# A Flamingo block in fp32: the resident operand's transfers issued from ScalarE's queue instead of SyncE's

## The chip, the core and the metric

The kernel runs on one core of one Trainium2 chip. The metric is the device time of one execution in microseconds (us); for each kernel the median of several executions is taken. A core has TensorE (matrix products, weights loaded by PEld), VectorE (DVE), ScalarE (ACT), GpSimd (POOL) and SyncE (SP). Each takes its own instructions strictly in order, and they wait for each other by semaphores. SP computes nothing: before the change every DMA of this kernel is issued from it. An engine that issues a DMA goes on to its next instruction once the transfer is handed over; the data land later and raise a semaphore.

## The reference

One gated cross-attention layer and one gated mixture of rank-16 experts, 16 batches of 128 rows, hidden size 1024, all fp32:

```python
x = x + tanh(g_xattn) * xattn(layernorm(x), ctx)
x = x + tanh(g_ffn) * ffn(layernorm(x))

# xattn: 32 query heads, 8 key/value heads, head size 128
q, k, v = hs @ q_w.T, ctx @ k_w.T, ctx @ v_w.T
q, k = rmsnorm(q, q_norm_w), rmsnorm(k, k_norm_w)
out = softmax(q @ k.T / sqrt(128) + mask) @ v     # per head
return out @ o_w.T

# ffn: top 16 of 64 experts
scores = xf @ Wr.T
gates = softmax of the 16 largest scores, 0 elsewhere
h = einsum('nd,krd->nkr', xf, A)
return einsum('nkr,kdr->nd', h * gates, B) * 2
```

## The kernel before

**Products.** Every large product is a Strassen-Winograd step: seven products of half-size blocks in place of eight. The work is a list of 100 entries, each with seven products, k = 0 to 6 (router entries have four). A product is four steps `at`, and each step three matmuls, since fp32 is split into a high part and a low rest: high by high, high by low, low by high (lines 719 to 721). One operand of an entry is **resident**: seven tiles `t_hi[k]`, `t_lo[k]` of 128 x 2048 numbers, which stay for a whole set of entries. The other is **staged**: `staged` (128 x 7 x 512) is loaded anew for every entry, four of its seven blocks are formed by POOL (`sums`, lines 1662 to 1668), and ACT or POOL (`s_hi`) and DVE (`s_lo`) split it.

**Sets.** There are eleven sets `tau` of resident tiles, so the resident operand is exchanged ten times. The set of an entry: 0 and 1 for entries 0 to 15 (keys and values), 2 and 3 for 16 to 47 (queries, with attention interleaved), 4 to 7 for 50 to 81 (output projection), 8 and 9 for 82 to 91 (router and expert inputs), 10 for 92 to 99 (expert outputs). The exchange happens while entries flow on. In the last entry of a set, `refill(e, k)` (line 384) waits until product k of that entry is done, since this was the last reader of tile k, and issues a 1 MB transfer of the next set's tile into `t_raw[k]`, which lies over `t_lo[k]`. `fill_t` then makes `t_hi[k]` on ACT (line 945, a cast) and `t_lo[k]` on DVE (line 1229, a subtraction). They stand at beats 4, 5, 6, 7, 9, 10 and 11 counted from the start of the last entry, a beat being one product: k = 0 is split while product 4 of the last entry runs. The first entry of the new set waits for `t_lo[k]` before its product k (line 713). There are 10 x 7 = 70 such refills.

**What else SP does.** `stage(e + 1, e)` (line 408) loads the staged operand of the next entry once `s_lo` of this entry is finished; it stands behind beat 1, so behind two refills, and in the query entries in round 1, behind three. Around it SP stores keys, values, combinations (`combos`), transposed rows (`xt`, `x2t`), attention heads and partial sums (`sums_out`), and loads them again. `sums_in` (line 509) waits until the store before has landed. SP's order is written out by hand in the loops from line 602: per beat `refill`, then `stage`, then the rest. In the query entries (line 624) a round is a quarter of an entry; rounds 0 to 3 hold refills 0; 1 and 2; 3 and 4; 5 and 6, each time ahead of `heads_out` and `stage`.

**What ACT does around it.** Keys and values (line 1138), output projection (line 1187) and the later loops: per beat the copies out of PSUM, `fill_s` (line 947, `s_hi` of the next entry at beats 5 and 6), then `fill_t`. In the query entries (line 1159), per round: `heads_copy`, the sums of squares of the queries, `exps`, `probs_high`, then `fill_t`. There `s_hi` is made by POOL.

Of the kernel before, what the change touches and what calls it, by code (L numbers as in the profile page):

```python
# [57 lines left out]
TAUS = 11  # L58
# [175 lines left out]
def program(nc, d, plan, bank, sem, ctx):  # L234

    m = Sbuf(nc)
    t_hi, t_lo, t_raw, s_hi, s_lo = [], [], [], [], []
# [145 lines left out]
    def _(sp):  # L383
        def refill(e, k):
            tau = entries[e].tau
            if plan.last_of_set[tau] != e or tau + 1 == TAUS:
                return
            tau += 1
            sp.wait_ge(prod, plan.prod[e, k])
            if tau in (2, 3):  # L390
                if k == 0:
                    sp.wait_ge(xt_out, 448 * (tau - 1))
                src = d.xt[tau - 2, k].rearrange("p k a c -> p k (a c)")
            elif tau in (8, 9):
                if k == 0:
                    sp.wait_ge(ft_out, 448 * (tau - 7))
                src = d.x2t[tau - 8, k].rearrange("p k a c -> p k (a c)")
            else:
                which = {1: 1, 4: 2, 5: 3, 6: 4, 7: 5, 10: 6}[tau]
                if k == 0:  # L400
                    sp.wait_ge(pc_out, 64 * which)
                if k in (0, 4, 5):
                    src = d.sets[which, {0: 0, 4: 1, 5: 3}[k]].rearrange("p (k c) -> p k c", k=4)
                else:
                    src = d.combos[which, {1: 0, 6: 1, 2: 2, 3: 3}[k]].rearrange("p (k c) -> p k c", k=4)
            sp.dma_start(t_raw[k][:, :, :], src).then_inc(t_in[k], 16)

# [194 lines left out]
        for e in range(KV0, QA0):  # L602
            for j in SEVEN:
                refill(e, entries[e].ks[j])
# [19 lines left out]
        for n in range(34):  # L624
            e = QA0 + n
            for r in range(4):
                if n < 32:
                    for k in ((0,), (1, 2), (3, 4), (5, 6))[r]:
                        refill(e, k)
# [18 lines left out]
        for q in range(32):  # L648
            e = O0 + q
            for j in SEVEN:  # L650
                refill(e, j)
# [17 lines left out]
        for e in range(A0, B0):  # L669
            s, idx = (e - A0) // 5, (e - A0) % 5  # L670
            for j, k in enumerate(entries[e].ks):
                beat = plan.beat0[e] + j
                refill(e, k)
# [267 lines left out]
    def _(act):  # L941
# [4 lines left out]

        def fill_s(e, ks):
# [190 lines left out]
        for e in range(KV0, QA0):  # L1138
            for j in SEVEN:
# [14 lines left out]
                if j == 5:  # L1154
                    key_squares(e, 0)
                    x_seeds(e)
                fill_t(plan.beat0[e] + j)

        for n in range(34):
            e = QA0 + n  # L1160
            for r in range(4):
# [19 lines left out]
                if 0 <= i - 2 < 128:  # L1181
                    probs_high(i - 2)
                for j in SLOT_BEATS[r]:
                    fill_t(plan.beat0[e] + j)
        heads_copy(127)

        for q in range(32):
            e = O0 + q
            for j in SEVEN:
# [7 lines left out]
                fill_s(e + 1, before_next(e, j))  # L1197
                fill_t(plan.beat0[e] + j)
# [620 lines left out]
```

## Time and profile before

| | |
|---|---|
| time, median of 3 executions | 2584.53 us (2575.5 to 2589.01) |
| the profiled execution's own time | 2579.23 us |
| its span in the trace | 2577.4 us |
| PE, DVE, POOL, ACT busy | 90%, 65%, 52%, 45% of the span |
| moved by DMA | 452.81 MB, mean 176 GB/s |
| granted TensorE clock, mean | 0.956 |

The trace is of one execution. Its times are counted from the start of the span. A row of a timeline that stands for several instructions ("x2") gives the first start and the time from there to the last end, waits between them included. The words in brackets are the idle time of the engine before the row and what ended it.

### The profile page before, as it was taken

Reading aid. Unit: us, or ns where it says so; the run is one execution under the profiler, and the core shown is the slowest. Engines: PE = TensorE matmul, PEld = TensorE weight load, DVE = VectorE, ACT = ScalarE, POOL = GpSimd, SP = SyncE. Lnnn points to the kernel's source line nnn. Section 1 sums busy time; section 2 is a strip of 40 time slices with the busy share of each in tenths; the row PEclk is TensorE's granted clock in tenths of the full one; section 3 lists DMA queues with packets and bytes.
Section 4 is the critical chain, followed back from the end, with each engine's and each line's share of the span. In section 5 each row is a group of like instructions: output and inputs, shape, how many; then the busy total and the mean of one; then the engine's idle time right before and its main releaser. Section 6 shows DMA issues by size and latency. Waiting matters only on the chain.

```text
span 2577.4 us, 35293 instructions
## 1 busy us (share of the span) xinstructions
PE 2328.8 (90%) x11384; PEld 1937.0 (75%) x11384; DVE 1664.1 (65%) x2655; ACT 1167.8 (45%) x3739; POOL 1343.0 (52%) x1822
## 2 busy tenths in 40 slices
PE   6997998999999999999996998999997576978899
PEld 4775786888888788888885886877875455756687
DVE  6557557777777787777776336556476555655755
ACT  4445445666666766666666333223231113332321
POOL 6888788555555555655554554322234443344431
PEclk8999999999999999999997999999998787989999
DMA  4788777322233522232334578576575548474754
GB/s 173 249 257 307 239 248 255 106 84 86 91 94 97 191 83 91 87 91 87 99 119 140 205 252 305 197 260 217 201 280 168 180 158 283 129 231 134 241 172 142
DMA packets 265541, 452.81 MB, mean 176 GB/s; under 512 B 14224, under 2 KB 154768, under 8 KB 249488
## 3 DMA queue, kind: packets, MB, share of 16 engines
q1 hardware_dynamic: 265360, 450.55, 52.7%
q8 instruction: 94, 1.54, 0.2%
q14 instruction: 87, 0.71, 0.1%
HBM read 288.49 MB, written 162.00 MB: 175 GB/s over the span
## 4 chain that ended last, share of the span: by engine, by line
PE 61%; DMA 13%; POOL 9%; DVE 9%; issue 4%; SPq 3%; ACT 1%; ACTq 0%; DVEq 0%; POOLq 0%
PE bank L719 16%; PE bank L721 16%; PE bank L720 16%; PE bank L777 4%; DVE s_lo L1229 2%; PE bank L785 2%; PE bank L765 2%; DVE t_lo L1229 2%; DMA gates_of_ranks<-gates_t 2%; SPq L537 2%; DMA x<-x_rows 1%; DVE x_rows L1377 1%; POOL staged L1664 1%; POOL staged L1662 1%; PE bank L800 1%
## 5 line engine op out<-in xcount | busy, mean ns | idle before, releaser
L719 PE MATMUL bank<-t_hi,s_hi 128*128 128x512 f32 x2720 | 1125.9, 414 | 160.2 <-DVE s_lo L1229 91.1
L721 PE MATMUL bank<-t_hi,s_lo 128*128 128x512 f32 x2720 | 1086.3, 399 | 0.0
L720 PE MATMUL bank<-t_lo,s_hi 128*128 128x512 f32 x2720 | 1085.4, 399 | 0.0
L719 PEld LDWEIGHTS bank<-t_hi,s_hi 128*128 128x128 f32 x2720 | 527.4, 194 | 278.8 <-DVE s_lo L1229 100.2
L1229 DVE TENSOR_TENSOR s_lo<-staged,s_hi 128x512 fp32r<-128x512 f32 x676 | 536.6, 838 | 212.8 <-ACT s_hi L954 203.5
L721 PEld LDWEIGHTS bank<-t_hi,s_lo 128*128 128x128 f32 x2720 | 525.8, 193 | 119.3
L720 PEld LDWEIGHTS bank<-t_lo,s_hi 128*128 128x128 f32 x2720 | 528.2, 194 | 94.5
L954 ACT CAST s_hi<-staged 128x512 fp32r<-128x512 f32 x452 | 258.6, 621 | 355.8 <-DMA staged<-heads 156.0
L1662 POOL TENSOR_TENSOR staged<-staged 128x512 f32<-128x512 f32 x96 | 135.3, 1410 | 441.8 <-DMA staged<-heads 249.4
L1243 DVE TENSOR_TENSOR sums<-sums,bank 128x512 f32<-128x512 f32 x184 | 125.1, 682 | 184.4 <-PE bank L721 165.0
L1647 POOL TENSOR_SCALAR q_v<-q_ss 128x4 f32<-128x4 f32 x128 | 44.2, 345 | 368.9 <-ACT q_seed L1038 365.8
L1229 DVE TENSOR_TENSOR t_lo<-t_raw,t_hi 128x2048 fp32r<-128x2048 f32 x77 | 190.5, 2482 | 50.7 <-ACT t_hi L945 41.4
L1339 DVE SCALAR_TENSOR_TENSOR probs<-bank,q_rstd,mask 128x128 f32<-128x128 f32 x512 | 144.1, 344 | 99.8 <-POOL q_rstd L1654 55.5
L1044 ACT ACTIVATE probs<-probs,neg_max 128x128 f32<-128x128 f32 x512 | 197.5, 387 | 15.3 <-DVE neg_max L1343 15.3
L1032 ACT ACTIVATE bank<-bank 128x128 f32<-128x128 f32 x512 | 136.4, 266 | 120.1 <-PE bank L765 120.0
L777 PEld LDWEIGHTS bank<-keys,queries 128*128 128x128 f32 x1024 | 136.9, 196 | 30.7 <-issue 20.4
L1026 ACT COPY heads<-bank 128x512 f32<-128x512 f32 x128 | 75.2, 587 | 178.4 <-PE bank L802 176.9
L777 PE MATMUL bank<-keys,queries 128*128 128x128 f32 x1024 | 139.3, 280 | 18.1 <-DVE probs L1339 18.1
L945 ACT CAST t_hi<-t_raw 128x2048 fp32r<-128x2048 f32 x70 | 132.8, 1907 | 32.4 <-DMA t_raw<-in_sets 22.1
L1664 POOL TENSOR_TENSOR staged<-staged 128x512 f32<-128x512 f32 x96 | 141.8, 1477 | 7.5
L1665 POOL TENSOR_TENSOR staged<-staged 128x512 f32<-128x512 f32 x96 | 144.0, 1500 | 0.0
L1668 POOL TENSOR_TENSOR staged<-staged 128x512 f32<-128x512 f32 x96 | 142.4, 1483 | 0.0
(137 smaller groups left out, 2865.2 us busy)
## 6 DMA issues: line engine op xcount, KB each, us to landing
sums<-sums SPq DMA_DIRECT2D x48, 1280.0 KB, 7.9
heads<-heads SPq DMA_DIRECT2D x128, 256.0 KB, 2.9
t_raw<-combos SPq DMA_DIRECT2D x24, 1024.0 KB, 12.0
staged<-in_w_q SPq DMA_DIRECT2D x32, 768.0 KB, 5.2
staged<-heads SPq DMA_DIRECT2D x32, 768.0 KB, 5.8
t_raw<-in_sets SPq DMA_DIRECT2D x22, 1024.0 KB, 10.1
x_rows<-in_x SPq DMA_DIRECT2D x32, 512.0 KB, 6.6
combo<-in_sets SPq DMA_DIRECT2D x15, 1024.0 KB, 6.4
```

The costliest lines, as they stand in the source:

```text
L719: nc.tensor.matmul(out[:, :], s_hi[w][:, cols], t_hi[k][:, at, :], start=start, stop=False, skip_group_check=True)
L720: nc.tensor.matmul(out[:, :], s_hi[w][:, cols], t_lo[k][:, at, :], start=False, stop=False, skip_group_check=True)
L721: done = nc.tensor.matmul(out[:, :], s_lo[w][:, cols], t_hi[k][:, at, :], start=False, stop=at == 3, skip_group_check=True)
L777: done = nc.tensor.matmul(bank[6][:, b * S:b * S + S], qt[j][:, b, :], kg[blk][:, b, :], start=True, stop=True)
L954: nc.scalar.copy(s_hi[k][:, :], staged[:, k, :]).then_inc(s_hi_done, 1)
L1044: done = nc.scalar.activation(pr[i % 3][:, b, :], pr[i % 3][:, b, :], ACT.Exp, bias=nmax[w][:, b:b + 1], accum_out=rsum[w][:, b:b + 1])
L1229: return nc.vector.tensor_tensor(out, whole, hi.bitcast(FP32), ALU.subtract)
L1339: done = nc.vector.scalar_tensor_tensor(pr[i % 3][:, b, :], bank[6][:, b * S:b * S + S], q_rstd[w][:, b:b + 1], mask[:, :], ALU.mult, ALU.add)
L1662: nc.gpsimd.tensor_tensor(staged[:, 2, :], staged[:, 3, :], staged[:, 6, :], ALU.add).then_inc(s_sum, 1)
L1664: nc.gpsimd.tensor_tensor(staged[:, 1, :], staged[:, 2, :], staged[:, 0, :], ALU.subtract).then_inc(s_sum, 1)
L1665: nc.gpsimd.tensor_tensor(staged[:, 3, :], staged[:, 0, :], staged[:, 3, :], ALU.subtract).then_inc(s_sum, 1)
L1668: nc.gpsimd.tensor_tensor(staged[:, 5, :], staged[:, 4, :], staged[:, 1, :], ALU.subtract).then_inc(s_sum, 1)
```

## The change

`refill` moves from SP's program to ACT's. The same 70 transfers with the same semaphores are issued by `nc.scalar.dma_start`, and the waits ahead of them (for the product, and for k = 0 also for the data's own store) are now ACT's. The place of each call: in the key/value, output and expert loops behind this beat's `fill_s` and right ahead of `fill_t`; in the query loop at the end of each round, behind `probs_high` and ahead of `fill_t`. The four loads of set 0 stay with SP. No computation changes.

```diff
     @block.sync
     def _(sp):
-        def refill(e, k):
-            ...
-            sp.wait_ge(prod, plan.prod[e, k])
-            ...
-            sp.dma_start(t_raw[k][:, :, :], src).then_inc(t_in[k], 16)
...
             for j in SEVEN:
-                refill(e, entries[e].ks[j])
                 if j == 1:
                     stage(e + 1, e)
...
             for r in range(4):
-                if n < 32:
-                    for k in ((0,), (1, 2), (3, 4), (5, 6))[r]:
-                        refill(e, k)
                 heads_out(4 * (n - 2) + r - 1)
...
     @block.scalar
     def _(act):
...
+        def refill(e, k):
+            tau = entries[e].tau
+            if plan.last_of_set[tau] != e or tau + 1 == TAUS:
+                return
+            tau += 1
+            act.wait_ge(prod, plan.prod[e, k])
+            if tau in (2, 3):
+                if k == 0:
+                    act.wait_ge(xt_out, 448 * (tau - 1))
+                src = d.xt[tau - 2, k].rearrange("p k a c -> p k (a c)")
+            ...
+            nc.scalar.dma_start(t_raw[k][:, :, :], src).then_inc(t_in[k], 16)
...
                     x_seeds(e)
+                refill(e, entries[e].ks[j])
                 fill_t(plan.beat0[e] + j)
...
                     probs_high(i - 2)
+                if n < 32:
+                    for k in ((0,), (1, 2), (3, 4), (5, 6))[r]:
+                        refill(e, k)
                 for j in SLOT_BEATS[r]:
                     fill_t(plan.beat0[e] + j)
...
                 fill_s(e + 1, before_next(e, j))
+                refill(e, j)
                 fill_t(plan.beat0[e] + j)
```

The SP queue in entry 31, the last query entry of set 2, before: `staged` is the next entry's operand, `xt` the source of the refills, `product` the semaphore of finished products.

```order
L406 DMA t_raw<-xt 128x2048 [waits product] x2
L485 DMA heads<-heads_172 128x2x256 [waits ot_copied]
L433 DMA staged<-in_w_q 128x3x512 [waits s_lo_done]
L434 DMA staged<-in_w_q 128x512
L406 DMA t_raw<-xt 128x2048 [waits product] x2
L485 DMA heads<-heads_173 128x2x256 [waits ot_copied]
L501 DMA values_raw<-values 128x512 [waits pv_done]
L406 DMA t_raw<-xt 128x2048 [waits product] x2
```

The same stretch of SP in the changed kernel (its line 409 is the old line 433):

```order
L461 DMA heads<-heads_172 128x2x256 [waits ot_copied]
L409 DMA staged<-in_w_q 128x3x512 [waits s_lo_done]
L410 DMA staged<-in_w_q 128x512
L461 DMA heads<-heads_173 128x2x256 [waits ot_copied]
L477 DMA values_raw<-values 128x512 [waits pv_done]
```

Three pairs of refills, each with waits for products, are gone from ahead of the staged load, the head stores and the value load.

ACT in rounds 2 and 3 of the same entry in the changed kernel (`q_ss`, `q_ln`, `q_seed` are the queries' norm, `probs` the softmax):

```order
L939 DMA t_raw<-xt 128x2048 [waits product] x2
L915 CAST t_hi<-t_raw 128x2048 [waits t_in0]
L915 CAST t_hi<-t_raw 128x2048 [waits t_in1]
L1020 COPY heads_172<-bank 128x512 [waits heads_out0,pv_done]
L1009 COPY queries_161<-bank 128x512 [waits s_done,product]
L1026 ACTIVATE bank,q_ss_109<-bank 128x128 [waits qt_done]
L1026 ACTIVATE bank,q_ss_109<-bank 128x128 x3
L1030 ACTIVATE q_ln_111<-q_ss_109,eps 128x4 [waits q_squared]
L1032 ACTIVATE q_seed_113<-q_ln_111 128x4 [waits q_logged]
L1038 ACTIVATE probs_170,row_sum_122<-probs_170,neg_max_120 128x128 [waits s_max]
L1038 ACTIVATE probs_170,row_sum_122<-probs_170,neg_max_120 128x128 x3
L1052 CAST probs_t_hi<-bank 128x512 [waits pv_done,pt_done]
```

The first row is new: refills 3 and 4 with their waits for products 3 and 4 now stand ahead of the casts of tiles 0 and 1 and of the whole of round 3. Another pair, 5 and 6, follows the last row, ahead of the cast of tile 2.

ACT in entry 65, the last one of set 5 (output projection), in the changed kernel:

```order
L939 DMA t_raw<-combos 128x2048 [waits product] x3
L939 DMA t_raw<-in_sets 128x2048 [waits product]
L915 CAST t_hi<-t_raw 128x2048 [waits t_in0]
L948 CAST s_hi<-staged 128x512 [waits staged_in,product]
L948 CAST s_hi<-staged 128x512 [waits s_sum,product]
L939 DMA t_raw<-in_sets 128x2048 [waits product]
L915 CAST t_hi<-t_raw 128x2048 [waits t_in1]
L948 CAST s_hi<-staged 128x512 [waits s_sum,product] x2
L939 DMA t_raw<-combos 128x2048 [waits product]
L915 CAST t_hi<-t_raw 128x2048 [waits t_in2]
```

Before, the casts stood in the same order without the DMA rows. Refill 4 now stands ahead of the cast of tile 0, refill 5 behind two `s_hi` that wait for the staged load and POOL's sum of it, refill 6 behind two more.

## Rows read from the trace of the kernel before

**Rows 1.** The page: busy time by engine; the chain that ended last.

```profile
PE 2328.8 (90%) x11384; PEld 1937.0 (75%) x11384; DVE 1664.1 (65%) x2655; ACT 1167.8 (45%) x3739; POOL 1343.0 (52%) x1822
...
PE 61%; DMA 13%; POOL 9%; DVE 9%; issue 4%; SPq 3%; ACT 1%; ACTq 0%; DVEq 0%; POOLq 0%
```

**Rows 2.** The tile t_raw: ns of an issue (min/median/max), waiters, landing times.

```profile
L406 SPq DMA_DIRECT2D t_raw<-combos x24: 319/430/5682, 196.7 to 2414.6; - x24
L406 SPq DMA_DIRECT2D t_raw<-in_sets x18: 333/432/2004, 196.1 to 2402.2; - x18
...
  ACT t_hi L945: 32.4, 16
...
DMA to landing us min/median/max: 4.6/10.9/17.3
```

**Rows 3.** Stretches: length, busy us of PE, PEld, DVE, ACT, POOL, clock, DMA share, GB/s.

```profile
821.85:851.18 29.33, 29.33 (x175) 25.50 (x174) 22.19 (x47) 18.82 (x82) 17.54 (x34) 1.00 0.29 90
...
883.38:922.37 38.99, 34.47 (x172) 28.85 (x173) 35.56 (x54) 24.34 (x76) 27.54 (x40) 0.87 0.29 92
...
1720.00:1748.00 28.00, 24.32 (x100) 19.44 (x99) 19.87 (x21) 14.54 (x13) 7.78 (x4) 0.94 0.95 368
```

**Rows 4.** Timeline of SP, entries 30 and 31: start us, us, what.

```profile
828.66 0.47 SPq L433 DMA_DIRECT2D staged<-in_w_q  x1
...
864.44 0.47 SPq L433 DMA_DIRECT2D staged<-in_w_q  x1
...
867.51 5.15 SPq L406 DMA_DIRECT2D t_raw<-xt  x2
...
875.54 5.13 SPq L406 DMA_DIRECT2D t_raw<-xt  x2
```

**Rows 5.** Timeline of POOL, entries 30 and 31.

```profile
839.81 1.30 POOL L1662 TENSOR_TENSOR staged<-staged 128x512 f32<-128x512 f32 x1
...
873.35 2.55 POOL L1662 TENSOR_TENSOR staged<-staged 128x512 f32<-128x512 f32 x1 [4.14 <-DMA staged<-in_w_q]
...
881.62 2.18 POOL L1674 CAST s_hi<-staged 128x512 fp32r<-128x512 f32 x3
```

**Rows 6.** Timeline of PE, the start of entry 32.

```profile
883.38 0.50 PE L719 MATMUL bank<-t_hi,s_hi 128*128 128x512 f32 x1 [2.62 <-DVE s_lo L1229]
...
887.21 2.05 PE L777 MATMUL bank<-keys,queries 128*128 128x128 f32 x8 [0.85 <-DVE probs L1339]
```

**Rows 7.** Timeline of ACT, the end of entry 31 and the start of 32.

```profile
870.03 3.72 ACT L945 CAST t_hi<-t_raw 128x2048 fp32r<-128x2048 f32 x2
...
878.32 1.91 ACT L945 CAST t_hi<-t_raw 128x2048 fp32r<-128x2048 f32 x1
...
887.82 0.40 ACT L1044 ACTIVATE probs<-probs,neg_max 128x128 f32<-128x128 f32 x1 [5.24 <-DVE neg_max L1343]
```

**Rows 8.** Timeline of POOL, entry 47.

```profile
1356.42 1.75 POOL L1662 TENSOR_TENSOR staged<-staged 128x512 f32<-128x512 f32 x1 [4.95 <-DMA staged<-heads]
```

**Rows 9.** Timeline of PE, the drain of the attention behind entry 47.

```profile
1369.48 2.05 PE L777 MATMUL bank<-keys,queries 128*128 128x128 f32 x8 [6.44 <-DVE probs L1339]
```

**Rows 10.** Timeline of SP, entries 65 and 66: staged load, load of the sums.

```profile
1720.79 0.37 SPq L433 DMA_DIRECT2D staged<-heads  x1
...
1733.60 0.32 SPq L515 DMA_DIRECT2D sums<-sums  x1
```

**Rows 11.** Timelines of POOL, PE and DVE in the same stretch, in this order.

```profile
1728.46 3.22 POOL L1662 TENSOR_TENSOR staged<-staged 128x512 f32<-128x512 f32 x1 [15.56 <-DMA staged<-heads]
...
1738.57 0.76 PE L719 MATMUL bank<-t_hi,s_hi 128*128 128x512 f32 x1 [2.81 <-issue]
...
1741.79 1.27 DVE L1243 TENSOR_TENSOR sums<-sums,bank 128x512 f32<-128x512 f32 x2
```

**Rows 12.** Timelines of ACT and PE, entries 86 and 87.

```profile
2287.47 0.62 ACT L954 CAST s_hi<-staged 128x512 fp32r<-128x512 f32 x1 [2.00 <-DMA staged<-in_w_r]
...
2289.73 0.50 PE L719 MATMUL bank<-t_hi,s_hi 128*128 128x512 f32 x1 [2.99 <-DVE s_lo L1229]
```

More of the change, by code:

```diff
@@ L383, in _ @@
     def _(sp):
-        def refill(e, k):
[L385 to L388, printed above, removed]
-            sp.wait_ge(prod, plan.prod[e, k])
[L390 to L405, printed above, removed]
-            sp.dma_start(t_raw[k][:, :, :], src).then_inc(t_in[k], 16)
         def stage(e, before):
@@ L650, in _ @@
             for j in SEVEN:
-                refill(e, j)
                 if j == 0 and q == 0:
@@ L672, in _ @@
                 beat = plan.beat0[e] + j
-                refill(e, k)
                 if j == 1:
@@ L945, in fill_t @@
                 nc.scalar.copy(t_hi[k][:, :, :], t_raw[k][:, :, :]).then_inc(t_hi_done, 1)
+        def refill(e, k):
[8 more added lines that the diff above has]
+                src = d.xt[tau - 2, k].rearrange("p k a c -> p k (a c)")
+            elif tau in (8, 9):
+                if k == 0:
+                    act.wait_ge(ft_out, 448 * (tau - 7))
+                src = d.x2t[tau - 8, k].rearrange("p k a c -> p k (a c)")
+            else:
+                which = {1: 1, 4: 2, 5: 3, 6: 4, 7: 5, 10: 6}[tau]
+                if k == 0:
+                    act.wait_ge(pc_out, 64 * which)
+                if k in (0, 4, 5):
+                    src = d.sets[which, {0: 0, 4: 1, 5: 3}[k]].rearrange("p (k c) -> p k c", k=4)
+                else:
+                    src = d.combos[which, {1: 0, 6: 1, 2: 2, 3: 3}[k]].rearrange("p (k c) -> p k c", k=4)
+            nc.scalar.dma_start(t_raw[k][:, :, :], src).then_inc(t_in[k], 16)
         def fill_s(e, ks):
@@ L1215, in _ @@
                 fill_s(e + 1, before_next(e, j))
+                refill(e, k)
                 fill_t(plan.beat0[e] + j)
```

## The prediction, made before the changed kernel ran

> **What bounds the kernel now.** I read the page first, by engine and by chain. PE is busy for 90% of the span and holds 61% of the chain; DMA has 13% of it and SP's queue 3% [rows 1]. So the time is PE's work plus places where PE waits, and the change can only act in ten of them, the exchanges of the resident operand. Second, the stretches. A plain query entry takes 29.33 us with PE busy throughout; entry 32, the first of set 3, takes 38.99, with DVE busy 35.56 and the clock at 0.87 in the place of 1.00 [rows 3]. An exchange costs PE some 10 us there, and DVE's splitting of the new tiles is most of the load. Third, the tile of the refills: ACT waits for landed refills 32.4 us in 16 of 70 cases, and a refill takes 10.9 us from issue to landing in the median, 4.6 at best [rows 2]. In most cases the refill is there before ACT asks. An earlier refill is therefore worth little; what counts is what stands behind the refills, on SP now and on ACT after the change. Fourth, the timelines at the exchanges: which wait ends last before PE's gap. At entry 32 it is `s_lo` of the staged operand (2.62 us), then the softmax (0.85) [rows 6], and `s_lo` waits for POOL's `s_hi` at 881.62, which follows POOL's sums, which waited 4.14 us for the staged load [rows 5].
>
> **Part 1: SP no longer waits for products ahead of the staged load (gain).** In entry 30, which starts at 821.85, the staged load is issued at 828.66, 6.81 us in; in entry 31, which starts at 851.18, at 864.44, 13.26 us in, since refills 1 and 2 wait for products 1 and 2 ahead of it [rows 3, 4]. Without them it goes at about 851.18 + 6.81 = 858.0, which is 6.4 us earlier. POOL started its sums 17.96 us into entry 30 (839.81); that point in entry 31 is 869.14, against 873.35 [rows 5]. So POOL starts 4.2 us earlier and has no other wait. PE can get back at most what it waits: 2.62 + 0.85 = 3.47 us [rows 6].
> Against it stands ACT's new wait. Refill 4 is the second of the pair that SP finished at 867.51 + 5.15 = 872.66; its product ended about 872.3. ACT's casts of tiles 0 and 1, which began at 870.03, must now wait for that and for the issue, and begin at 872.7, 2.7 us later [rows 4, 7]. Likewise refill 6 was finished at 875.54 + 5.13 = 880.67, so the cast of tile 2 moves from 878.32 to about 881. Behind it on ACT are the head copy and the norms of the next round; POOL's norm and DVE's softmax wait for those. ACT has 5.24 us of idle time before 887.82 that takes the delay in [rows 7]. I take 3.0 us gained of the 3.47, as the cover is longer than the delay; bounds 0 (ACT's order eats it) and 6 (the low clock behind the gap, 0.87 in that stretch, goes as well).
> Entry 47 has the same form: POOL waits 4.95 us for the staged load, and PE then 6.44 us for the softmax [rows 8, 9]. Here the attention drains behind it, and ACT and DVE share the chain, so I take 2.5 us; bounds 0 and 5. In the other eight exchanges SP's wait for product 1 ends before `s_lo` of the running entry does, so nothing comes from this.
>
> **Part 2: the queue ahead of the staged load (gain in one place, open in the others).** In entry 87 ACT's `s_hi` waits 2.00 us for the staged load and PE 2.99 us behind that [rows 12]. Two refills, one store and one load of the gates stand ahead of it in SP's order; without the refills I take 2.0 us, bounds -2 (a loss) and 3. In entries 7, 15, 57, 65, 73, 81 and 91 the staged load also stands behind refills 0 and 1, but there it isn't clear what happens. In entry 65 it is issued at 1720.79 and POOL starts on it at 1728.46, 7.67 us later [rows 10, 11]. The DMA engines are busy 0.95 of the time there and move 368 GB/s [rows 3]: they have no room, and what one transfer gains another loses. Before, refill 1 is ahead of the staged load and refills 2 to 4 behind it. After, refill 1 shares with it, and so do 2 to 4. The trace has only one queue that moves data, so how two share is in no row. I take 0: one refill less ahead, one or two more beside it. One refill at 368 GB/s is 1.05 MB / 368 = 2.85 us; with that per exchange as the bound either way, the ends are -2.85 x 7 = -20 and +20 us, and the rivals below are those ends.
> The store and reload of the sums behind the staged load are the same question: the reload is issued at 1733.60 and DVE's addition, the first that needs it, starts at 1741.79, 8.19 us later [rows 10, 11], so it has no slack that I can count on.
>
> **Part 3: ACT pays for the issue (loss).** An issue of a refill holds SP's queue 0.43 us in the median, 5.68 at most [rows 2]. 70 x 0.43 = 30 us move to ACT. ACT is busy 45% [rows 1], and refills 0 to 3 fall where it waits for PE anyway, so most are hidden. Refill 4 is ahead of the cast of tile 0 and refill 5 ahead of that of tile 1, which leads to `t_lo` and to PE's product 1, late by 2.81 us already in entry 66 [rows 11]. One issue per exchange on the path, in the seven exchanges where ACT has no such cover: 7 x 0.43 = 3.0 us. Bounds: 0, if DVE is what PE waits for, and 12, if two of them count (6.0) and one takes the longest 5.68.
> The refills 4 to 6 of entry 65, which SP issued late since `sums_in` held it until 1733.60, can go with their products; ACT's own order puts 5 and 6 behind the staged operand. I count 0 for this, as most refills are early.
>
> **The sum.** -3.0 - 2.5 - 2.0 + 3.0 = -4.5 us. Against the profiled execution's own 2579.23 (span 2577.4 and 1.8 around it) this is 2574.7; the median of the runs shown is 5.3 higher, and the predicted median is 2584.5 - 4.5 = 2580.0.
>
> **Rival 1, slower: refills overtake.** If a queue of its own lets the refills through beside or ahead of the staged load, one more of them passes before it lands: 2.85 us later. The chain from there is known: POOL's sums, `s_hi`, cast of tile 1, `t_lo`, PE's product 1, where PE waits already (2.81 us) [rows 11]. At all exchanges but 3 and 4: 8 x 2.85 = 22.8, and 2580.0 + 22.8 = 2603; half of it, 2591, where the engine shares evenly. It decides from the first 0.1 us of delay on where PE waits already. For it: 0.95 busy DMA [rows 3], and refills that are mostly early and would be earlier still for nothing. Against it: refill 5 cannot be issued before the staged load has landed, since ACT is in order, so the pressure stops by itself.
> The Trainium skill, "DMA: Bandwidth & Descriptors", section "Queues, rings and completion order", says that an engine takes turns between its queues packet by packet. If so, a queue with large packets would get more than its half beside one with small ones, which speaks for this rival; no row here has two data queues.
>
> **Rival 2, faster: the staged load comes clear.** If the two share evenly by bytes and the refill ahead no longer counts, the staged load is up to 2.85 us earlier at exchanges 1, 2, 5, 6, 7 and 10, capped by gaps like 2.81 [rows 11], so about 2.4 each: 14.4, giving 2565.6. For it: POOL waits for exactly this load in all exchanges shown [rows 5, 8, 11]. Against it: DVE is busy 35.56 of 38.99 us behind it [rows 3], and would take the gain back.
>
> **Rival 3: no gain, only the issue.** ACT's waits for products eat part 1, and what is left is part 3: 2584.5 + 3.0 = 2587.5.
> The Trainium skill, same page, section "Issuing engines are not separate DMA queues", says that issuing from several engines saves only the sequencer's issue time. By it part 2 is 0 throughout and no bandwidth is won; it leaves part 1, which is order and not bandwidth, as it is.
>
> **Chances.** The forecast (2572 to 2588) 0.35, rival 3 0.15, rival 1 0.25, rival 2 0.25. A measurement of this kernel tells some 0.5% from no change, 12.9 us, so 2571.6 and 2597.5 are the limits. Faster: rival 2 nearly whole and a little of the forecast (part 1 at its upper bounds), 0.29. Slower: rival 1 with more than half of its price, and part 3 at its worst, 0.24. Within: 0.47. The range leaves a tenth out on each side: from 2562 (rival 2 with part 1 at its bounds) to 2603 (rival 1 in full).
>
> **What the changed profile would show.** Part 1: in entries 31 and 47 POOL's line 1662 starts about 18 us into the entry, PE's gap before entry 32 is under 1 us, ACT's pair of casts starts near 872.7. Part 2: the time from staged issue to POOL's start in entry 65, 7.67 before; over 9 is rival 1, under 6 rival 2. Part 3: the new ACT queue rows last 0.4 us; if many last several us, the issue itself is the cost. What would make me wrong: DMA issues on ACT that stall on SP's, or head stores and reloads that become late in the plain entries too.

## The result and the profile of the changed kernel

The changed kernel takes 2613.02 us in the median (2608.4 to 2617.58), the kernel before 2580.26 us beside it: ratio 1.0128, 95% interval [1.0107, 1.0150]. It is 1.3% slower, some 33 us. I had predicted 2580.0 us and a range of 2562 to 2603, so both the likeliest case and the range were wrong. The forecast was counted from 2584.5 us, the median known then; counted from the 2580.26 measured here its -4.5 us would have meant 2575.8. The profiled execution took 2615.66 us, its span 2613.5.

The page of the changed kernel: busy time by engine, queues (packets, MB, share of the 16 DMA engines), and the chain.

```profile
PE 2335.7 (89%) x11384; PEld 1942.6 (74%) x11384; DVE 1667.8 (64%) x2655; ACT 1165.2 (45%) x3739; POOL 1357.6 (52%) x1822
...
q1 hardware_dynamic: 255280, 377.15, 44.5%
q10 hardware_dynamic: 10080, 73.40, 7.4%
...
PE 57%; DMA 15%; DVE 10%; POOL 9%; issue 4%; SPq 4%; ACT 2%; ACTq 0%; DVEq 0%; POOLq 0%
```

Against [rows 1] the engines' own work is nearly the same (PE +6.9 us, POOL +14.6, DVE +3.7, ACT -2.6). The chain moves from PE (61% to 57%) to DMA (13% to 15%) and to the engines that wait for it; the reload of the sums alone holds 5% of it by the page, and isn't named in the chain of the kernel before. The refills are now a queue of their own, q10: 73 of 451 MB in packets of 8 KB.

The tile of the refills: ns of an issue, who waited for its writers, landing times.

```profile
L939 ACTq DMA_DIRECT2D t_raw<-combos x24: 325/332/382, 198.0 to 2445.4; - x24
L939 ACTq DMA_DIRECT2D t_raw<-in_sets x18: 334/339/423, 194.5 to 2444.2; - x18
...
L939 ACTq DMA_DIRECT2D t_raw<-x2t x14: 325/326/963, 2162.2 to 2322.8; - x14
...
  ACT t_hi L915: 3.3, 1
...
DMA to landing us min/median/max: 4.7/7.6/14.9
```

The change does to the refills what one could wish [rows 2]: no issue is long (0.33 us in the median), they land after 7.6 us and not 10.9, and ACT waits for landed refills 3.3 us and not 32.4. Yet the kernel is slower. What became slower is what else moves on SP's queue while refills are under way. The sum tiles, in the kernel before and in the changed one (two answers; the first line of each is DVE's wait for the reload):

```profile
  DVE sums L1243: 17.7, 11
...
DMA to landing us min/median/max: 5.3/7.9/11.7
```

```profile
  DVE sums L1243: 26.4, 12
...
DMA to landing us min/median/max: 5.3/8.4/19.2
```

The longest landing of a staged load went in the same way from 13.8 to 19.8 us. I dated each entry by the first matmul of its first product and took the difference to the kernel before, profile against profile, of the last entry of a set and the entries behind it. The experiments e1 to e11 are explained in the next section; their kernels stand beside it. In us:

| exchange (entries) | changed | e1 | e2 | e3 | e4 | e5 | e6 | e9 | e10 | e11 |
|---|---|---|---|---|---|---|---|---|---|---|
| none (0 to 6) | +3.1 | +3.4 | +2.4 | +3.2 | -3.6 | +2.8 | +2.9 | +2.5 | -1.6 | +1.2 |
| 1 (7, 8) | +6.8 | -0.2 | +5.5 | +0.3 | +0.2 | +4.1 | +3.1 | +4.6 | -0.1 | +2.3 |
| none (9 to 14) | -0.1 | -0.6 | -1.9 | -0.7 | +1.8 | -0.5 | -7.8 | -4.8 | -0.1 | -9.7 |
| 2 (15, 16) | +2.6 | +2.3 | +8.2 | +2.5 | +1.8 | +5.5 | +0.5 | +3.6 | +1.5 | 0.0 |
| 3 (31, 32) | -2.8 | -3.1 | 0.0 | +0.4 | -2.8 | -4.7 | -1.4 | -2.9 | +0.3 | -2.8 |
| 4 (47 to 56) | -5.1 | -6.8 | -2.1 | -0.9 | -5.2 | -6.3 | -3.0 | -4.5 | -2.5 | -4.9 |
| 5 (57 to 59) | +1.0 | -1.5 | +3.3 | -2.7 | -1.9 | -0.5 | -0.7 | -2.0 | +0.6 | -1.5 |
| 6 (65 to 67) | +8.6 | +0.7 | +6.5 | +2.2 | +0.6 | +2.7 | +1.5 | +2.8 | +1.3 | +0.1 |
| 7 (73 to 75) | +7.1 | -0.3 | +5.2 | +0.6 | +1.0 | +3.4 | -1.0 | +2.8 | -0.8 | -1.3 |
| 8 (81 to 83) | +5.3 | -0.7 | +3.2 | -0.4 | +0.9 | +0.7 | -0.1 | +4.1 | +0.1 | +2.5 |
| 9 (86 to 90) | +0.8 | +0.6 | +3.9 | -2.1 | +2.0 | +2.1 | +1.8 | +2.0 | +1.8 | -1.3 |
| 10 (91 to 93) | +6.6 | +0.2 | +6.4 | +0.8 | 0.0 | +7.2 | +1.6 | +4.9 | -1.0 | -2.2 |

The two rows marked "none" hold no exchange: what differs there, up to 4 us in the first and up to 10 in the second, tells how far one profile can be trusted, so a single row of 1 to 3 us shows nothing. The sums over many rows and the medians carry the argument. The plain entries that are not in the table agree with the kernel before within 1 us each stretch in the changed kernel. In the changed kernel the two query exchanges gain 7.9 us and the other eight lose 38.8.

**Exchange 10, where a landing is the whole loss.** Timelines of SP, ACT's queue, POOL and PE in the changed kernel, entry 91 (it starts at 2410.12):

```profile
2421.52 0.36 SPq L409 DMA_DIRECT2D staged<-gated  x1
```

```profile
2414.99 0.34 ACTq L939 DMA_DIRECT2D t_raw<-in_sets  x1
...
2417.49 5.77 ACTq L939 DMA_DIRECT2D t_raw<-combos  x3
...
2425.66 0.34 ACTq L939 DMA_DIRECT2D t_raw<-in_sets  x1
```

```profile
2441.12 1.26 POOL L1662 TENSOR_TENSOR staged<-staged 128x512 f32<-128x512 f32 x1 [20.18 <-DMA staged<-gated]
```

```profile
2442.99 0.79 PE L689 MATMUL bank<-t_hi,s_hi 128*128 128x512 f32 x1 [11.93 <-DVE s_lo L1229]
```

And the same two points in the kernel before (SP, then POOL; entry 91 starts at 2380.56):

```profile
2391.96 0.36 SPq L433 DMA_DIRECT2D staged<-gated  x1
```

```profile
2404.99 1.26 POOL L1662 TENSOR_TENSOR staged<-staged 128x512 f32<-128x512 f32 x1 [13.61 <-DMA staged<-gated]
```

The staged load is issued 11.40 us into the entry in both. From there POOL gets it after 2404.99 - 2391.96 = 13.03 us before and 2441.12 - 2421.52 = 19.60 us after: 6.57 us, the whole of the exchange's loss. Refills 0 to 4 (one, three and one) are issued by 2425.66 on the other queue and run beside the staged load. Before, refills 0 and 1 stood ahead of it and 2 to 4 behind it in the same queue. What the engines moved from 2420 to 2429 in the changed kernel (queue: packets, MB, share):

```profile
DMA packets 1612, 3.68 MB, mean 409 GB/s; under 512 B 67, under 2 KB 1234, under 8 KB 1238
...
q10 hardware_dynamic: 407, 3.06, 82.2%
q1 hardware_dynamic: 1205, 0.61, 22.5%
```

The engines are full, and SP's queue, which has stores, loads of rows and gates and the staged load to move, gets 0.61 MB of 3.68, or 17%. At most four of its 1205 packets here are of 2 KB or more (1238 are under 8 KB, 1234 under 2 KB): seven us after its issue the staged load, whose packets have 2 KB, has hardly begun, since the 512 byte stores ahead of it are still on their way. By 2433.5 the refills are nearly through (ScalarE's queue moves 0.06 MB from there to 2441.1), and SP's queue moves the rest alone. So the loss is made while the refills run, in stores that the staged load stands behind.

**Exchange 1, where the staged load is issued late.** Here seven stores of transposed rows stand ahead of it on SP. Their issues, in the kernel before and in the changed one:

```profile
189.04 6.94 SPq L474 DMA_DIRECT2D xt<-x_columns  x7
```

```profile
192.33 13.96 SPq L450 DMA_DIRECT2D xt<-x_columns  x7
```

ScalarE issues refill 0 at 194.52, refill 1 at 197.99 and two more by 205.40, so they run beside these stores, and SP's issues take twice as long. The staged load is issued 197.49 - 188.00 = 9.49 us into entry 7 before and 206.34 - 191.25 = 15.09 us after, and POOL starts 9.70 and 11.64 us later. Together that is 7.5 us more, and entry 7 is 7.5 us longer. A second queue can thus cost not only a landing but also the issue, since SP hangs on stores that drain slowly.

**Exchanges 5 to 7, where the sums come on top.** (The last store of sums goes in entry 74 and the last reload in entry 80, so exchange 8 has neither.) SP in entries 73 and 74 of the changed kernel (staged load, store of the sums, reload of the sums), then DVE and PE:

```profile
1896.18 0.37 SPq L409 DMA_DIRECT2D staged<-heads  x1
...
1897.24 0.32 SPq L483 DMA_DIRECT2D sums<-sums  x1
1912.47 0.32 SPq L491 DMA_DIRECT2D sums<-sums  x1
```

```profile
1922.91 0.69 DVE L1243 TENSOR_TENSOR sums<-sums,bank 128x512 f32<-128x512 f32 x1 [4.61 <-DMA sums<-sums]
...
1924.72 2.28 DVE L1229 TENSOR_TENSOR t_lo<-t_raw,t_hi 128x2048 fp32r<-128x2048 f32 x1
```

```profile
1927.11 0.77 PE L689 MATMUL bank<-t_hi,s_hi 128*128 128x512 f32 x1 [6.30 <-issue]
```

SP issues the reload only when the store has landed. That took 1912.47 - 1897.24 = 15.23 us; before it took 9.78 (issued at 1882.41, reload at 1892.19). DVE works in order: its addition waits 4.61 us for the reload, and the `t_lo` behind it is late. PE then waits 6.30 us; the profile names no releaser for this ("issue"), but that `t_lo` ends at 1927.00 and PE starts at 1927.11. In the kernel before DVE had no such wait in this place:

```profile
1901.62 1.27 DVE L1243 TENSOR_TENSOR sums<-sums,bank 128x512 f32<-128x512 f32 x2
```

The same chain stands in entries 58 and 66. In entry 58 it costs 8.0 us, of which 6.4 come back in entry 59, where PE no longer waits for the staged operand; this is why exchange 5 stands at +1.0 only.

The staged load suffers here as well, and mostly in its second piece, the transfer of 256 KB that is issued 0.4 us behind the first. It lands after 14.9 us in entry 65 (7.9 before) and 10.4 in entry 73 (7.3 before), while the first piece of entry 73 lands after 7.7 us (7.1 before).

### The profile page after: what moved, and what is told of

The parts are those of the page before. It is cut to its first block, busy times and chain, and to the rows that moved or that the text cites. A ratio compares the mean times of both kernels' runs of the same rounds, so it can differ in the third digit from the quotient of the medians.

```text
span 2613.5 us, 35293 instructions
## 1 busy us (share of the span) xinstructions
PE 2335.7 (89%) x11384; PEld 1942.6 (74%) x11384; DVE 1667.8 (64%) x2655; ACT 1165.2 (45%) x3739; POOL 1357.6 (52%) x1822
## 4 chain that ended last, share of the span: by engine, by line
PE 57%; DMA 15%; DVE 10%; POOL 9%; issue 4%; SPq 4%; ACT 2%; ACTq 0%; DVEq 0%; POOLq 0%
PE bank L689 15%; PE bank L691 15%; PE bank L690 15%; DMA sums<-sums 5%; PE bank L747 4%; DVE s_lo L1229 3%; PE bank L755 2%; DVE t_lo L1229 2%; PE bank L735 2%; SPq L513 2%; DMA gates_of_ranks<-gates_t 1%; DMA staged<-in_ctx 1%; DVE x_rows L1377 1%; DMA x<-x_rows 1%; DMA x2t<-x_columns 1%
## 5 line engine op out<-in xcount | busy, mean ns | idle before, releaser
L1662 POOL TENSOR_TENSOR staged<-staged 128x512 f32<-128x512 f32 x96 | 134.0, 1396 | 455.9 <-DMA staged<-heads 254.8
L1647 POOL TENSOR_SCALAR q_v<-q_ss 128x4 f32<-128x4 f32 x128 | 51.3, 401 | 369.0 <-ACT q_seed L1032 365.8
L1674 POOL CAST s_hi<-staged 128x512 fp32r<-128x512 f32 x224 | 148.2, 701 | 0.0
L1665 POOL TENSOR_TENSOR staged<-staged 128x512 f32<-128x512 f32 x96 | 146.9, 1530 | 0.0
L1668 POOL TENSOR_TENSOR staged<-staged 128x512 f32<-128x512 f32 x96 | 143.1, 1490 | 0.0
```

The source lines that it names most:

```text
L1665: nc.gpsimd.tensor_tensor(staged[:, 3, :], staged[:, 0, :], staged[:, 3, :], ALU.subtract).then_inc(s_sum, 1)
L1668: nc.gpsimd.tensor_tensor(staged[:, 5, :], staged[:, 4, :], staged[:, 1, :], ALU.subtract).then_inc(s_sum, 1)
L1674: nc.gpsimd.tensor_copy(s_hi[k][:, :], staged[:, k, :]).then_inc(s_hi_done, 1)
```

## The experiments

**Theory O:** in SyncE's one queue a staged load or a store passes only what was issued before it. With the refills on a second queue, those issued later run beside it, and since DMA is full in the exchanges they take its time. **Rival A:** ScalarE's waits and issues hold up its casts. The expectations of e1 to e4 call theory O by the name S; the letters P and Q, C and D, R and N are explained where they come up. The ratios below are to the kernel before on the same chip.

**e1: only exchanges 3 and 4 from ScalarE.** ScalarE's copy of the helper has these lines, and SyncE keeps its own with the other eight sets in them:

```
+            if tau not in (3, 4):
+                return
```

> Only the refills of the two exchanges in query entries 31 and 47 go from ScalarE's queue; the other eight stay on SyncE. Theory S (the loss of the full change comes from refills on a queue of their own that take transfer time from SyncE's staged loads and stores, in the exchanges outside the query entries; the gain of freeing SyncE is real): these two exchanges alone showed -2.8 and -4.9 us in the full change, so 7.7 us faster than before, ratio 0.997. Rival A (the loss is ScalarE's: its waits for products and its issues hold up its casts, in every exchange): no gain, ratio 1.000 to 1.003. Rival N (the gains seen in the two entries are one-off differences of one profile): ratio 1.000.

Measured: 0.9979 [0.9966, 0.9992], 2574.84 against 2580.64 us, -5.8. The direction holds, the size is three quarters of what I expected. The profile has -3.1 and -6.8 in these two exchanges; elsewhere it differs by no more than the rows without an exchange do (+3.4 in entries 0 to 6, +2.3 in exchange 2).

**e2: the complement.** The same two lines with the sets exchanged.

> The complement: the eight other exchanges from ScalarE's queue, those of query entries 31 and 47 on SyncE as before. Theory S: all of the loss and none of the gain, so the full change's +33 us and the missing 7.7 us: +40 us, ratio 1.0155. Rival A: the loss is in proportion to the exchanges, +26 us, ratio 1.010. Rival N: the same as the full change, +33 us, ratio 1.0128.

Measured: 1.0144 [1.013, 1.0158], 2618.9 us, +38.3, near the 40 that I expected. So the loss is in the eight and the gain in the two, and they add: -5.8 + 38.3 = 32.5, against 32.8 for the change.

**e3: ScalarE's waits without its transfers.** The kernel before, and in ScalarE's code at the places of the change:

```
+            act.wait_ge(prod, plan.prod[e, k])
```

> All transfers are issued by SyncE as before; ScalarE has only the seventy waits for products at the places where the full change issues, and no transfer. Theory S: within 2 us of before, ratio 1.000. Rival A (the place in ScalarE's order, where it waits for a product before the next cast): most of the loss is here, +20 to +33 us, ratio 1.008 to 1.013.

Measured: 1.0003 [0.9993, 1.0012]. Rival A falls as far as the waits for products go. (The change also has ScalarE wait, for k = 0, for the data's own store; e3 doesn't, and no run parts this.) That ScalarE is held by a product before its next cast costs nothing here. I take it that its casts would have waited for PE or DVE anyway, but no run shows this.

**e4: one queue, other order.** SyncE's code of a query entry:

```
-                if n < 32:
-                    for k in ((0,), (1, 2), (3, 4), (5, 6))[r]:
-                        refill(e, k)
                 heads_out(4 * (n - 2) + r - 1)
...
                     stage(plan.next(e), e)
...
+                if n < 32:
+                    for k in ((0,), (1, 2), (3, 4), (5, 6))[r]:
+                        refill(e, k)
```

> All transfers stay on SyncE, but in query entries each refill is written behind the store of heads, the staged load and the group loads of its quarter, not ahead of them. One queue, other order. If the gain in entries 31 and 47 comes from the staged load no longer standing behind a wait for a product, it comes without a second queue: 7.7 us faster, ratio 0.997 (theory S). If it needs the second queue (the refills themselves landing earlier), ratio 1.000, or slower by up to 5 us where a refill now lands late.

Measured: 0.9979 [0.9967, 0.999], 2574.58 us, -6.1. The gain in entries 31 and 47 (-2.8 and -5.2) is the same as that of the change, without a second queue. It came from SP's order alone. The edit puts the refills behind the head stores and the value loads as well as behind the staged load, and doesn't part these three.

**e5 and e6: smaller packets, on ScalarE and on SyncE.** The refill in two transfers, and the count for which the cast waits doubled:

```
-            nc.scalar.dma_start(t_raw[k][:, :, :], src).then_inc(t_in[k], 16)
+            for h in range(2):
+                nc.scalar.dma_start(t_raw[k][:, h:4:2, :], src[:, h:4:2, :]).then_inc(t_in[k], 16)
```

> The full change, but each 1 MB refill is written as two transfers of every second row of 512 values, so that a packet of a refill has 2,048 bytes, not 8,192. Theory P (while two queues are both loaded the engines take packets from each in turn, so the queue with the larger packets gets the larger share: 8,192 bytes against 2,048 for a staged load): the staged loads and the sums get a much larger share and most of the loss of 33 us is gone, ratio 1.000 to 1.006. Theory Q (the loss comes from a second loaded queue as such, whatever its packets): no change from the full change, ratio 1.011 to 1.014.

> The control of the run before: refills on SyncE as in the kernel before, in the same two transfers of 2,048 byte packets. One queue, so no shares: both theories expect within 0.2% of before, at most 70 further issues of some 0.04 to 0.4 us beside the products; ratio 0.999 to 1.002. If small packets themselves cost transfer time, it is slower, and that amount is to be taken off the run before.

Measured: e5 1.0069 [1.0045, 1.0093], 2598.93 us; e6 1.0027 [1.0012, 1.0043], 2586.36 us. Both miss by a little: e5 is above 1.006 and the control above 1.002. (An issue on SP takes 0.32 us at the least in the kernel before; the 0.04 of the expectation stands in no row.) Of the 32.8 us the change costs, 12.6 are left between the two (2598.93 - 2586.36), so packet size is a large part of it. The same stretch of entry 91 as above, in e5 (2403 to 2412):

```profile
DMA packets 2961, 3.53 MB, mean 392 GB/s; under 512 B 126, under 2 KB 1621, under 8 KB 2961
...
q10 hardware_dynamic: 1388, 2.68, 77.1%
q1 hardware_dynamic: 1573, 0.85, 30.8%
```

SP's queue has 0.85 of 3.53 MB, 24% and not 17%. Its packets there are the 512 byte ones of the stores that stand ahead of the staged load, so the refills' packets are still four times as large, and exchange 10 gets nothing back (+7.2, landing 19.8 us). Exchanges 6 to 8, whose staged loads have 2,048 byte packets and whose sums (in 6 and 7) 10,240, lose 6.8 and not 21.0 us.

The Trainium skill, "DMA: Bandwidth & Descriptors", section "Queues, rings and completion order", says that an engine takes turns between its queues packet by packet. The direction agrees. If the records' packets were those of the rule, their counts would be equal while both queues are loaded: in e5 they nearly are (1573 to 1388), in the changed kernel they are 1205 to 407, three small ones for each large one, so the traces do not show the rule as it stands.

**e7 and e8: the sums' traffic cut to a fifth, with the refills on ScalarE and on SyncE.**

```
-            sp.dma_start(d.sums[q % 8], acc[q % 2][:, :, :]).then_inc(acc_out[q % 2], 16)
+            sp.dma_start(d.sums[q % 8][:, 0:1, :], acc[q % 2][:, 0:1, :]).then_inc(acc_out[q % 2], 16)
```

and the reload in the same way. Four of the five columns are neither stored nor reloaded, so this part of the computation isn't done.

> The full change with the store and the reload of the partial sums cut to the first of their five columns of 512 (0.26 MB, not 1.31 MB, each way; the other four columns are left out of store and reload, so this part of the computation isn't done). To be read against the next run. Theory C (in the exchanges of entries 57, 65, 73 and 81 the price is the chain store of sums, reload, first add, product of the next entry, slowed by the refills): its excess over the next run is 12 to 18 us instead of 33 to 36, since the terms of entries 58, 66, 74 and 83 (8.0, 6.6, 4.1 and 2.4 us) go. Theory D (the staged load alone is the price, the sums only stand beside it): its excess stays 30 us or more.

> The kernel before, refills on SyncE, with the same cut of the sums' store and reload to one column in five. The base of the run before. Less traffic ahead of staged loads and refills: between 0 and 12 us faster than before, ratio 0.995 to 1.000.

Measured: e7 0.9999 [0.9982, 1.0016], 2579.59 us; e8 0.992 [0.9896, 0.9945], 2559.66 us, which is more than the 12 us I allowed. Most of that lies in the plain entries 76 to 80, which are 15.4 us shorter in e8 and 14.7 in e7, so it falls out of the difference between the two. The excess is 19.9 us and not 32.8: between the two theories, nearer to C, which had said 12 to 18. By the entries, exchanges 5 to 7 lose 16.7 us in the changed kernel and 5.3 between e7 and e8 (+1.4, +2.7, +1.2), so some 11 us goes with the sums. Exchange 8, which has no sums to move, keeps its loss (+5.3 and +4.1), though the expectation had counted 2.4 us of it as theirs. The rest I put down to the staged load; these are differences of single profiles, good to a few us. DVE's wait for the reload, 26.4 us in the changed kernel, is 0.8 in e7:

```profile
  DVE sums L1275: 0.8, 1
```

**e9: later refills held back.** The changed kernel, and in ScalarE's helper:

```
+            if entries[e].ks.index(k) >= 2:
+                act.wait_ge(st12_in, 16 * (plan.order[plan.next(e)] + 1))
```

> The full change, but in every exchange ScalarE's refills from the third on also wait until the staged load of the next entry has landed; the first two go as in the full change. Theory O (the loss comes from refills that in the kernel before stood behind the staged load in SyncE's queue and now run beside it): the staged load takes 8 to 10 us from issue to the first sum again, also in the exchange of entry 91 (19.6 us in the full change, 13.0 before); the refills land later than before, which gives part back; ratio 1.000 to 1.006. Rival R (a second queue slows the other whatever runs beside the staged load, or the loss is in the refills themselves): ratio 1.011 to 1.016, and more if ScalarE's further wait costs.

Measured: 1.004 [1.002, 1.0061], 2590.05 us against 2578.94, so 11.1 us are left of the 32.8. The staged load is back: 11.85 us in entry 91, 5.8 to 9.1 in entries 7, 15, 57, 65 and 73. (In entry 7 it is still issued late, 13.3 us in and not 9.5, as refills 0 and 1 run beside SP's seven stores here too.) What is left comes at least in entry 91 from the wait that I added, and not from the second queue. DVE's `t_lo` waits 91.5 us in all, most of it for ACT's casts, 59.7 in the changed kernel (the two answers on the tile t_raw, e9 first):

```profile
  DVE t_lo L1262: 91.5, 22
```

```profile
  DVE t_lo L1229: 59.7, 23
```

ACT waits for landed refills only 10.1 us in e9, so it isn't late landings that hold most of the casts. In entry 91 ACT stands in its new wait until 2413.4. Only behind it come the copy out of PSUM, the cast of tile 0, whose refill was issued at 2393.26, and the split of the staged operand. ACT, then PE:

```profile
2414.79 1.90 ACT L946 CAST t_hi<-t_raw 128x2048 fp32r<-128x2048 f32 x1
2416.59 0.62 ACT L981 CAST s_hi<-staged 128x512 fp32r<-128x512 f32 x1
```

```profile
2421.69 0.79 PE L720 MATMUL bank<-t_hi,s_hi 128*128 128x512 f32 x1 [12.38 <-DVE s_lo L1262]
```

POOL has the staged load 24.28 us into this entry (24.43 in the kernel before), and still the next entry starts 6.9 us later.

**e10: only the first two refills of an exchange from ScalarE.** SyncE's copy returns for `entries[e].ks.index(k) < 2`, ScalarE's for the others.

> Only the first two refills of each exchange (in the query entries as well) go from ScalarE's queue; the other five stay on SyncE, behind the staged load as in the kernel before. SyncE then has no wait for a product ahead of the staged load anywhere. Theory O: the gain of the two query exchanges stays (some -2 us each, since the first three refills stood ahead there) and two refills beside the staged load cost no more than two ahead of it: ratio 0.996 to 1.001. Rival R (any refill on a second queue costs, in proportion two sevenths of 40 us): ratio 1.003 to 1.006.

Measured: 1.0 [0.9988, 1.0012]. Two refills beside the staged load cost no more than two ahead of it. In the eight exchanges it sums to +3.4 us, in the changed kernel to +38.8. In the query entries the gain is mostly gone. The expectation was wrong there: the second round holds refills 1 and 2, refill 2 stayed on SP, and the staged load still stood behind its wait for a product (issued 13.3 us in).

**e11: one queue, the second refill behind the staged load everywhere.** e4, and in the other three loops of SyncE:

```
-                refill(e, k)
                 if j == 1:
                     stage(e + 1, e)
+                refill(e, k)
```

(in the output entries it also stands behind the store of the sums).

> One queue, order alone: in the query entries as in the run that wrote refills behind each quarter's other transfers, and in all other entries the second refill is written behind the staged load and the store of sums, not ahead of them. Theory O: the 5.6 us of that run, and up to 2.85 us (one 1 MB refill at 368 GB/s) more in each exchange where the staged load is late, entries 7, 15, 57 and 91: ratio 0.994 to 0.998. Rival: the second refill is then late for its cast instead, and only what was gained stays: 0.998; or it is slower, 1.000.

Measured: 0.9945 [0.9928, 0.9961], 2564.25 us against 2578.94, 14.7 us faster than before and 1.8% faster than the change. It beats both kernels. The staged load in entries 57, 65 and 73 takes 5.7 to 5.9 us and not 7.2 to 7.7; in exchange 10 10.64 and not 13.03. SP and POOL there:

```profile
2377.72 0.36 SPq L433 DMA_DIRECT2D staged<-gated  x1
```

```profile
2388.36 1.26 POOL L1662 TENSOR_TENSOR staged<-staged 128x512 f32<-128x512 f32 x1 [11.22 <-DMA staged<-gated]
```

By the table the query exchanges give 7.7 us, exchange 10 2.2, and 9.7 come in entries 9 to 14, which hold no edit: in the kernel before PE waits three times there for the norm of keys on POOL, 8.4 us in all (3.54, 3.47, 1.43), and in e11 2.1 us. e6, which does not move the refills, has 7.8 of the 9.7 too, so I do not put this part down to the order. What the order beyond e4's gives is thus shown only for the landing times, and about 2 us in exchange 10.

**e12: exchange 10 alone.** e1's two lines with the set (10,).

> Only the refills of the last exchange (entry 91) go from ScalarE's queue, the other nine stay on SyncE. In the full change this exchange took 6.6 us more, with the staged load landing 19.6 us after its issue, not 13.0, behind SyncE's stores of 512 byte packets. If each exchange carries its own loss (theory O: local competition between the two queues), the staged load takes 19 to 20 us again and the kernel is 6 to 7 us slower, ratio 1.0025. If the loss in the last exchange comes from what the nine exchanges ahead of it left behind, the staged load takes 13 us and the ratio is 1.000.

Measured: 1.0032 [1.0015, 1.0048], 2588.31 against 2580.62 us, +7.7. The exchange shows +6.9 in the profile and the staged load takes 2413.96 - 2393.97 = 19.99 us. SP, then POOL:

```profile
2393.97 0.36 SPq L435 DMA_DIRECT2D staged<-gated  x1
```

```profile
2413.96 1.26 POOL L1696 TENSOR_TENSOR staged<-staged 128x512 f32<-128x512 f32 x1 [20.56 <-DMA staged<-gated]
```

Seven transfers moved to the other queue, nothing else: this exchange carries its own loss, whatever the others do.

## Why the prediction was wrong, point by point

**Part 1, the order ahead of the staged load, was right.** I had said that POOL starts 18 us into entry 31 and that PE's gap before entry 32 falls under 1 us. Entry 31 of the changed kernel starts at 864.21; POOL and PE there:

```profile
882.20 1.30 POOL L1662 TENSOR_TENSOR staged<-staged 128x512 f32<-128x512 f32 x1
```

```profile
894.26 0.50 PE L689 MATMUL bank<-t_hi,s_hi 128*128 128x512 f32 x1 [0.41 <-DVE s_lo L1229]
```

That is 17.99 us, and 0.41 us in place of 2.62 [rows 6]. The terms were -3.0 and -2.5; measured are -2.8 and -5.1 in the profile, and the medians of e1 and e4 give -5.8 and -6.1 for the two together. Entry 47's term was half of what the profile shows: PE's wait of 6.44 us [rows 9] came to 3.69, the rest of the drain got 1.3 us shorter in place of taking the gain back, and 1.0 us comes in entries 50 to 56. The casts of tiles 0 and 1 did move by the 2.7 us that I had worked out (885.77 is 21.56 us into the entry, before it was 18.85 [rows 7]), and cost nothing, as said. ACT and PE there and in the drain:

```profile
885.77 3.71 ACT L915 CAST t_hi<-t_raw 128x2048 fp32r<-128x2048 f32 x2 [2.60 <-PE bank L691]
```

```profile
1377.64 2.04 PE L747 MATMUL bank<-keys,queries 128*128 128x128 f32 x8 [3.69 <-DVE probs L1339]
```

**Part 2 is the step that failed, in its "I take 0".** I had the mechanism as rival 1 and gave it a quarter. Measured are +38.8 us in the eight exchanges (+38.3 in the medians, e2). Four things in it were wrong.
First, the count of what passes. I argued that "one refill less ahead, one or two more beside it" cancel, and that "the pressure stops by itself" because ACT is in order. In entry 91 five refills were issued before the staged load landed, one as each product ended. ACT's order held back only the last two. e9 held back five of seven, and the staged load landed as before; e10 left two, and the loss in these exchanges went.
Second, the price. I bounded an exchange by one refill, 2.85 us. Exchange 10 alone costs 6.6 to 7.7 us (table, e12), the eight together 38.8 and not 22.8, so the range ended at 2603 with the result at 2613. The bound priced a queue by the bytes of one transfer, while the loss is made over the whole time in which refills run beside it: SP's queue had 17% of the bytes there, and the stores ahead of the staged load were slowed with it.
Third, the sums. I wrote of their reload that it "has no slack that I can count on" and then gave it no term of its own. It has two landings in a row, store and reload, and e7 and e8 put some 11 of the 16.7 us of exchanges 5 to 7 on it.
Fourth, the issue. I took the staged load's issue time as given, and in entry 7 it came 5.6 us later into the entry, behind stores that SP took 13.96 us to issue, in entry 86 5.0 us later.
My own mark, over 9 us from staged issue to POOL in entry 65 in place of 7.67 [rows 10, 11], came out at 12.26, and pointed to rival 1. The mark was a weak one: the same time is 8.52 us in e2, which has the whole loss, and 9.22 in e3, which has none of it.

**Entry 87's term** (-2.0, from [rows 12]) had the wrong sign. PE's wait at the start of entry 87, 2.99 us before, is in the changed kernel:

```profile
2323.62 0.79 PE L689 MATMUL bank<-t_hi,s_hi 128*128 128x512 f32 x1 [9.01 <-DVE s_lo L1229]
```

ACT's `s_hi` waits 10.61 us for the staged load there, in place of 2.00. It was issued 16.59 us into entry 86 and not 11.54, behind a load of gates that took SP 6.33 us to issue. Entry 86 is 5.1 us longer, and 4.0 to 5.8 in e2 and e5, but within 0.8 in e1, e3, e4, e6 and e10. Entries 87 and 88 give 4.3 us of it back, so exchange 9 as a whole (+0.8 here, -2.1 to +3.9 in the other kernels) isn't settled. Exchange 2 isn't settled either: its +2.6 is also in e1 and e3, where its refills stay on SyncE.

**Part 3** was of the right kind and small. An issue on ACT takes 0.33 us and not 0.43, none was long, and e3 prices the waits at nothing. The issues alone were not measured apart; e1, with fourteen of them, stands within 0.5 us of e4, which has none. Rival 3 (2587.5) falls with that, and rival 2 (2565.6) with the staged loads, which outside the query entries came later and not earlier.

The Trainium skill's rule "Issuing engines are not separate DMA queues" (same page), that several issuing engines save sequencer time only, isn't contradicted for bandwidth: the kernel moved the same 453 MB at a mean of 173 GB/s, 176 before. (409 GB/s in the stretch above and 368 in that of [rows 3] are stretches with different packets, so they don't compare.) It doesn't tell the time: which transfer gets the bandwidth changed, and with it 33 us.

**The sum again.** -7.9 in the two query exchanges, +38.8 in the eight and +2.1 in all plain entries between them: +33.0. A further 3.1 stand in the first entries, ahead of any refill; e1 and e3 show them as well, so they aren't the change's. The medians differ by 32.8. What stays open: how the engines share between the two queues (a ratio of packets of 3 to 1 in one kernel and 1.1 to 1 in the other), how exchanges 5 to 7 part into staged load and sums beyond the rough 5 and 11, what exchange 8 loses its 5.3 us by, and why entries 9 to 14 are at times 8 to 10 us shorter.

## What to carry to other kernels

One queue is also a priority: what the critical path needs must be issued ahead of bulk transfers, and a queue of its own for the bulk gives that up, above all where the bulk has the larger packets and DMA is full. Before moving a transfer to another queue, list all that stays behind (here staged loads, and a store whose landing releases a reload) and price each by the share it will get as long as the bulk runs, not by one transfer's length; count too the issues that stall behind it. If an in-order engine waits for a product ahead of an urgent issue, first change the order on that same engine: three moved lines (e4) brought the gain here, and without the loss.

## What the runs showed of the hardware

- With 8,192 byte packets on ScalarE's queue and mostly 512 byte ones on SyncE's, both loaded, SyncE's moved 0.61 of 3.68 MB in 9 us, 17%; with 2,048 byte packets against them 0.85 of 3.53 MB, 24%.
- A staged load of 1 MB behind 512 byte stores took 13.0 us with two refills ahead of it in one queue, and 19.6 to 20.0 us with refills on the other queue, alone (e12) as in the whole change.
- Seventy issues on ScalarE took 0.33 us in the median and 0.96 at most, while SyncE's took up to 5.68 us in the kernel before. In the changed kernel SyncE's issues still stall: seven stores of 256 KB took 13.96 us to issue in entry 7, 6.94 before, and the staged load behind them 3.82 us.

```profile
206.34 3.82 SPq L409 DMA_DIRECT2D staged<-in_ctx  x1
```

- Splitting each 1 MB refill in two transfers of 2,048 byte packets made the kernel 0.27% [0.12, 0.43] slower in one queue (e6).
